# Nine block products split once more, with their inner weight sums made in the first group

## What is computed

```python
# layer 0: one weight for all batches, a low-rank addition chosen by the batch's first id
x = x + (einsum('bsi,oi->bso', x, weight) + bias
         + scale[:, None, None] * einsum('bsr,bor->bso', einsum('bsi,bri->bsr', x, a_sel), b_sel))
# layer 1: the whole weight (2048 x 2048) is chosen by the batch's second id, out of 16
x = x + einsum('bij,bkj->bik', x, w1[id_b])
```

## Time and profile before

| | us |
|---|---|
| median of three runs | 2757.64 |
| the profiled execution | 2755.91 |
| its span in the trace | 2754.1 |
| TensorE busy (share of the span) | 2713.4 (99%) |
| VectorE busy | 1836.7 (67%) |
| ScalarE busy | 1339.2 (49%) |
| GpSimd busy | 732.9 (27%) |
| DMA, mean over the span | 234 GB/s |

### The profile page before, as it was taken

One profiled execution on the slowest core, in us unless ns is written; L12 is line 12 of the kernel. 1 busy time (PEld: TensorE's weight loads), 2 busy tenths in 40 slices (PEclk: granted clock), 3 DMA queues, 4 the chain that ended last, 5 costly groups with the idle time before them and its releaser, 6 DMA issues.

```text
span 2754.1 us, 34174 instructions
## 1 busy us (share of the span) xinstructions
PE 2713.4 (99%) x12042; PEld 2244.8 (82%) x12042; DVE 1836.7 (67%) x1631; ACT 1339.2 (49%) x1409; POOL 732.9 (27%) x589
## 2 busy tenths in 40 slices
PE   6999999999999999999999999999999999999999
PEld 5788888888888888888888888888888888888887
DVE  5766776866655657686656575768675656667865
ACT  3332355756533335576643232666664323366665
POOL 4435812411512111141251210113134122111421
PEclk9999999999999999999999999999999999999999
DMA  7858947666855435666794544899997554499997
GB/s 269 331 188 284 351 167 225 206 222 219 312 173 198 143 129 178 211 221 208 232 310 161 185 156 137 288 305 312 308 326 276 168 180 163 138 303 311 309 321 246
DMA packets 197627, 645.17 MB, mean 234 GB/s; under 512 B 23216, under 2 KB 33616, under 8 KB 197456
## 3 DMA queue, kind: packets, MB, share of 16 engines
q1 hardware_dynamic: 197456, 642.98, 68.6%
HBM read 651.28 MB, written 58.72 MB: 258 GB/s over the span
## 4 chain that ended last, share of the span: by engine, by line
PE 89%; POOL 3%; DMA 3%; DVE 3%; ACT 1%; issue 1%; SPq 0%; POOLq 0%; ACTq 0%; DVEq 0%
PE acc L820 16%; PE acc L821 16%; PE acc L822 16%; PE acc L766 13%; PE acc L777 13%; PE acc L767 13%; DMA raw<-w 3%; POOL raw L493 2%; PE acc L739 2%; DVE ws L710 1%; POOL raw L476 1%; PE acc L775 1%; DMA raw<-xt 0%; DVE ops L710 0%; ACT ws L574 0%
## 5 line engine op out<-in xcount | busy, mean ns | idle before, releaser
L710 DVE TENSOR_TENSOR ws<-raw,ws 128x1024 fp32r<-128x1024 f32 (+1 forms) x1008 | 1317.5, 1330 | 432.9 <-ACT ws L574 428.8
L574 ACT CAST ws<-raw 128x1024 fp32r<-128x1024 f32 (+1 forms) x1008 | 1027.9, 1044 | 1146.7 <-PE acc L777 519.0
L820 PE MATMUL acc<-ws,ops 128*128 128x512 f32 (+1 forms) x2048 | 799.0, 390 | 5.2 <-DVE ws L710 4.8
L821 PE MATMUL acc<-ws,ops 128*128 128x512 f32 (+1 forms) x2048 | 797.9, 390 | 0.0
L822 PE MATMUL acc<-ws,ops 128*128 128x512 f32 (+1 forms) x2048 | 797.9, 390 | 0.0
L766 PE MATMUL acc<-ops,ws 128*128 128x512 f32 x1792 | 702.1, 392 | 19.8 <-DVE ops L710 14.4
L777 PE MATMUL acc<-ops,ws 128*128 128x512 f32 x1792 | 700.9, 391 | 0.0
L767 PE MATMUL acc<-ops,ws 128*128 128x512 f32 x1792 | 699.8, 391 | 0.0
L493 POOL TENSOR_TENSOR raw<-raw,eye_s 128x128 f32<-128x128 f32 x384 | 351.6, 946 | 1261.3 <-DMA raw<-w 1261.3
L820 PEld LDWEIGHTS acc<-ws,ops 128*128 128x128 f32 x2048 | 384.6, 188 | 89.1 <-issue 6.5
L476 POOL TENSOR_TENSOR raw<-raw 128x1024 f32<-128x1024 f32 (+1 forms) x116 | 305.6, 2636 | 555.1 <-DMA raw<-xt 456.5
(11 more groups left out here) (61 smaller groups left out, 651.4 us busy)
## 6 DMA issues: line engine op xcount, KB each, us to landing
raw<-w SPq DMA_DIRECT2D x928, 512.0 KB
raw<-xt SPq DMA_DIRECT2D x176, 512.0 KB
raw<-w_sums SPq DMA_DIRECT2D x104, 512.0 KB
out<-ost SPq DMA_DIRECT2D x128, 256.0 KB, 6.0
w_sums<-raw SPq DMA_DIRECT2D x32, 512.0 KB, 5.3
x_sums<-raw SPq DMA_DIRECT2D x16, 512.0 KB, 4.2
raw<-x_sums SPq DMA_DIRECT2D x16, 512.0 KB
raw<-a SPq DMA_DIRECT2D x80, 64.0 KB
```

Of the source, the lines that this page charges most:

```text
L574: ins = eng.copy(hi, src)
L710: ins = eng.tensor_tensor(lo, src, hi, ALU.subtract) if hi is not None else eng.tensor_copy(lo, src)
L820: eng.matmul(acc, yh, wh, start=begin, stop=False)
L821: eng.matmul(acc, yh, wl, start=False, stop=False)
```

## The change

For `k` in `TWO` = (2, 3, 5) of groups 1, 2 and 3 (nine block products in all) the block product is itself done by seven smaller products `s` of a 2 x 2 form. A small product takes two weight tiles' worth of slots (`("V", g, k, s, hh)`, `hh` = 0, 1); each block has 24 matmuls of 128 x 128 by **256** columns. A product that was 8 blocks of 24 matmuls of 512 columns becomes 14 blocks of 24 matmuls of 256 columns. The low-rank matmuls stay 16 per product (four each within `s` = 1, 2, 6 and four in a new block `LV`).

```diff
+            if two(g, k):
+                for s in range(7):
+                    for hh in range(2):
+                        blocks.append(("V", g, k, s, hh))
+                    if s == 5:
+                        blocks.append(("LV", g, k))
+                continue
...
+                    for o in range(2):
+                        dst = acc[:, 512 * hh + 256 * o:512 * hh + 256 * o + 256]
+                        for t in range(4):
...
+                            eng.matmul(dst, wh, xh, start=fresh, stop=False, skip_group_check=True)
+                            eng.matmul(dst, wh, xl, start=False, stop=False, skip_group_check=True)
...
+                            ins = eng.matmul(dst, wl, xh, start=False, stop=(t == 3), skip_group_check=True)
```

**The inner input sums** are four tiles of 128 x 1024 per product (`("XT", g, k, m)`). POOL makes them in place, from the four raw tiles of the product's X splits, which therefore stay in `raw` until the sums have been split; ACT and DVE split them into the other half of `ops`, once the block product before is done:

```diff
+        return (["T3", "T2"], ["T1"], [], ["T4"])[index[2]]
...
+                elif kind == "XT":
+                    g, k, m = index
+                    x11, x21 = raw[:, 0:2, 0:512], raw[:, 0:2, 512:1024]
+                    x12, x22 = raw[:, 2:4, 0:512], raw[:, 2:4, 512:1024]
+                    if step == "T3":
+                        eng.wait_ge(s_lo, max(number["X", g, k, b] for b in range(G)) + 1)
...
+                        ins = eng.tensor_tensor(x12, x22, x12, ALU.subtract)
```

```diff
+    begin = ts[at["S", 0, 0, 0, 0, 0]]
+    for i, k in enumerate(TWO):
+        for o in range(4):
+            key = begin + 8.0 + 26.0 * (4 * i + o)
+            jobs.append((key, key, "P", (k, o)))
+            for step in range(len(pool_steps("P", (k, o)))):
+                pool_at["P", k, o, step] = key + 3.0 * step
```

**The evictions** of such a product are nine additions of 128 x 1024 (task `evt`: PSUM is now four pairs of banks) instead of eight of 128 x 512:

```diff
+        pair = [ctx.enter_context(nc.psum_tensor(f"acc{i}", [P, 1024], F32)) for i in range(4)]
...
+                    eng.tensor_tensor(dst, acc, src, ALU.add).then_inc(s_ev0, 1)
```

More of the change, by code:

```diff
@@ L9 @@
 ALU = mybir.AluOpType
+ACTF = mybir.ActivationFunctionType
 P = 128
@@ L33, with two @@
 SAVE_AFTER = 5
+TWO = (2, 3, 5)
+def two(g, k):
+    return g > 0 and k in TWO
 def plan_blocks():
@@ L129, in pool_steps, with halves @@
     return []
+def halves():
+    main, first = {}, 0
+    for g in range(NG):
+        half = first
+        for k in range(K):
+            if k and not two(g, k - 1):
+                half = 1 - half
+            main[g, k] = half
+        first = 1 - half
+    return main
 def program(nc, xt, a0, w0, w1, bt, bias, row, col, seq, half, scal, eye, out):
@@ L139, in program @@
         now += LORA_COST if b[0] == "W" and b[2] in (2, 3, 5) else 0.0
+        now += LORA_COST if b[0] == "V" and b[3] in (1, 2, 6) else 0.0
         te.append(now)
-    slots = [b for b in blocks if b[0] in ("W", "LA", "S")]
+    slots = [b for b in blocks if b[0] in ("W", "V", "LA", "S")]
     slot_of = {b: n for n, b in enumerate(slots)}
+    main_half = halves()
     def slot_done(n):
@@ L180, in program @@
                 key = free + 0.3 + (need - free) * (b + 0.2) / 4.6
-                splits.append((key, need, "X", (g, k, b)))
+                jobs.append((key, need, "X", (g, k, b)))
+            if two(g, k):
+                free = te[other_done(g, k)]
+                ready = key + 2.8
+                for m in range(4):
+                    for step, what in enumerate(pool_steps("XT", (g, k, m))):
+                        pool_at["XT", g, k, m, step] = ready
+                        ready += 2.6
+                    jobs.append((max(ready + 0.1, free + 0.4 + 2.6 * m), ts[at["V", g, k, 3 + m, 0]], "XT", (g, k, m)))
         for h in range(2):
@@ L224, in program @@
             split_of[r] = (n, i, what)
[L225 to L233, removed]
+    dadd_no = {number_at["W", 0, 1, o]: o + 1 for o in range(HT)}
     def out_no(g, h, kc, b):
         return ((g * 2 + h) * C1 + kc) * G + b
+    scalar_tasks, vector_tasks, stores = [], [], []
@@ L238, in program, with last_ev @@
+    scalar_tasks.sort(key=lambda t: t[:2])
+    vector_tasks.sort(key=lambda t: t[:2])
+    stores.sort()
+    ev_no = {}
+    for _, _, what, index in vector_tasks:
+        if what in ("ev0", "evt"):
+            ev_no[index] = len(ev_no) + 1
+    def last_ev(g, k, o):
+        return ev_no[g, k, 4 if o < 4 else 8] if two(g, k) else ev_no[g, k, o, 0]
     with ExitStack() as ctx:
@@ L388, in save @@
             def save(n):
-                kind, index = splits[n][2:4]
-                r, _ = saves[n]
+                kind, index = jobs[n][2:4]
                 if n in dadd_no:
@@ L413, in _ @@
                             eng.wait_ge(s_pool, pool_no[m, j])
-                    else:
-                        eng.wait_ge(s_lo, m + 1)
-                        if m in saves:
-                            eng.wait_ge(s_save[place[r]], saves[m][1])
-                if what[0] not in ("w0", "scratch", "t2") and not ordered:
+                    elif kind == "X" and two(*index[:2]):
+                        eng.wait_ge(s_lo, max(number["XT", index[0], index[1], i2] for i2 in range(4)) + 1)
+                    else:
+                        eng.wait_ge(s_lo, number[(kind, *index)] + 1)
+                    if prior[r] in saves:
+                        eng.wait_ge(s_save[place[r]], saves[prior[r]])
+                if what[0] not in ("w0", "scratch", "t2", "w2") and not ordered:
                     ordered = True
@@ L453, in _ @@
                     eng.dma_start(bias_s[:], bias).then_inc(s_const, 16)
-                if n in saves and i + 1 == len(raws[n]):
+                if (saved(kind_, index_) or kind_ == "P") and i + 1 == len(raws[n]):
                     waiting.append(n)
@@ L499, in split_views @@
         def split_views(n):
-            kind, index = splits[n][2:4]
+            kind, index = jobs[n][2:4]
+            if kind == "XT":
+                g, k, m = index
+                i = HT * (1 - half_of(g, k)) + 4 * (m // 2)
+                l, c = ((0, 0), (2, 512), (2, 0), (0, 512))[m]
+                v = raw[:, l:l + 2, c:c + 512].rearrange("p l (t n) -> p t l n", t=4)
+                c = 256 * (m % 2)
+                hi, lo = (ops[:, i:i + 4, w, c:c + 256].rearrange("p t (l n) -> p t l n", l=2) for w in range(2))
+                return [(v, hi)], [(v, hi, lo)]
             if kind == "BS":
```

406 lines of the change are left out of this document (302 added, 104 removed).

## The result

The changed kernel takes 2919.15 us (median of 4 runs, 2917.39 to 2919.69), the kernel before 2757.8 in the same comparison: 1.0585 times as long, 95% interval 1.0567 to 1.0604. The forecast was slower, 2789, with a range to 2832; the loss is five times as large, 161 us for 31.

A forecast was written before the change was run, and what follows sets the result against it. TensorE bounds the old kernel; in split products DVE, with POOL beside it, would. Waits of 60.3 us less 28.8 saved give +31.5 on 2755.9, 2787.4; with 1.7 for the median, 2789 us, range 2724 to 2832.

The forecast's parts named there:

- TensorE: what goes: Split products: 336 matmuls of 256 columns at 0.12 us save 3.2 us each; nine save 28.8, between 2 and 49.
- DVE: what comes, and POOL beside it: Split products: DVE work 38.1 us (k=3) or 45.7 (k=2, 5), plus 1.4 stolen per POOL operation, 11.2 per product.
- The sum: DVE work plus stolen time less 7.9 us, against TensorE's time: 20.1 us of waits per group, 60.3 over three.
- the 7.9 us: How far DVE may fall behind TensorE, by the ring of `ws`, once per run of split products.
- break-even: The whole change breaks even where each POOL operation steals c from DVE: 24c - 13.1 = 9.6 us per group, c = 0.95.
- DVE hides: Rival: in split products POOL operations cost DVE under 0.5 us each, TensorE stays the bound; 2729 us, chance 0.23.
- The rest: ACT, loads, P jobs, first group's slots, stores and new orders outside the split products' sum: hidden or taken as 0.
- The P jobs: Twelve weight-sum jobs, 48 POOL operations, 62 us in some 350, and 25 MB of transfers: hidden, at most some 8 us.
- slots of `raw` bound: Rival: some 20 loads per split product through five slots take up to 51.6 us; +54 over nine, 2812, chance 0.08.

The follow-up runs named there:

- experiment 15: Changed kernel with only k=3 split once more, no P jobs, X's `raw` slots lent to weight loads; 2763.51 us, 1.0028 times the kernel before.
- e14_k3_alone: The run of experiment 15: changed kernel with only k=3 split once more, no P jobs, X's `raw` slots lent; 2763.51 us, 1.0028 times the kernel before.
- the frame: Changed kernel with its new `raw` slots, three output tiles and new orders, but no product split once more and no P jobs; 2788.82 us, 1.0125 times the kernel before.
- e6_lend: The frame with X's four slots of `raw` lent to weight and rank-16 weight loads too; 2760.3 us, 1.0018 times the kernel before.
- e12_best: Changed kernel with X's slots lent, stores earlier, P jobs' POOL steps and saves 6 us later, and `LV` last; 2889.82 us, 1.0484 times the kernel before.
- the frame with the P jobs: The frame plus the twelve P jobs (loads, POOL operations, saves), no product split once more; 2856.87 us, 1.0379 times the kernel before.
- e11_no_xt_sums: Changed kernel without the P jobs (inner weights read from plain weights) and without POOL's four XT sums per product; 2807.65 us, 1.0179 times the kernel before.

## Why the prediction was wrong, step by step

- *TensorE: what goes.* Right. 0.12 us per small matmul, 3.2 us won per product. The bounds were 0.1133 and 0.129; the nearest row was the spacing of two weight loads in the earlier trace rows.
- *DVE: what comes, and POOL beside it.* Right in kind: DVE with POOL beside it fills 93% of k=2 and 3. The eviction at 1.23 was 1.21, the time stolen per POOL operation at 1.4 was 1.3 there and 1.0 in k=5. But eight such operations were counted in each product, and k=2 and 3 have twelve together, k=5 has four. The stolen time was priced at 22.4 and 11.2 us and is 16.0 and 3.9.
- *The sum.* It gave 98.3 us for k=2 and 3 and 49.0 for k=5; measured in group 1 are 99.1 and 50.6. That they meet so closely is luck, for its terms did not hold. In k=2 and 3 DVE is busy for 92.7 us and idle for 6.4, mostly in waits for casts. The busy time is less than the sum's 106.2 because 6.4 us less were stolen and because splits that follow each other start 1.14 us apart though each is 1.22 long (two take 2.28 in the chain shown for experiment 15). The idle time was set at nothing. And the 7.9 us by which DVE was allowed to fall behind do not appear: TensorE waits for an eviction at `LV`, 13.3 of its 19.9 us of waits, and only 6.6 for the low parts in `ws` and `ops`, where the forecast put them all. Over the nine products the net was put at +31.5 and is +42.2. `e14_k3_alone` shows the same from the other side: where the sum says that TensorE stays the bound, it is 2.5 to 4.1 us short.
- The break-even in the rival *DVE hides* has a slip: its own terms give 24c - 13.5, not 13.1, and c = 0.96.
- *The rest* is the step that failed. "The first group has no such products ... it may lose as much again or win it, taken as 0": measured +31.0 in the changed kernel and +22.5 in the frame. It is the slots: with X's lent, the frame loses nothing there (`e6_lend`) and the whole change 1.7 us (`e12_best`). A tile of k=1 takes three of five slots at a time, and that could be counted beforehand.
- The P jobs were "hidden", with at most 8 us: measured +66.5. They were priced as amounts (62 us of POOL in 350, 25 MB of DMA). In the frame with the P jobs, where the loss is 68.9, POOL's time is 14 of it and all that is left at the end 5. What the prediction left out is what stands behind a wait in its queue: SP's wait for POOL before a save, and the stores placed by a fixed planned distance behind it, are 49 us, the stores most of them.
- The blocks around the split products were put at 0 and lose 19.1 us, 8.9 of them by POOL's XT sums before the `LA` splits (by `e11_no_xt_sums`).
- The rival *slots of `raw` bound* had the right object in the wrong place: it priced the split products, where the wait for the next X operand does show in `e14_k3_alone`, and not the first group.

## What to carry to other kernels

A job put beside other work is priced by the queues it stands in, not by its busy time: name for each wait that it adds the engine that issues it and everything issued after it. When a pool of buffers is parted by use, count for each stage how many one item takes at once. And when TensorE's work is cut at the price of more splitting, count for each stage which operations of POOL really fall into it, add the time that DVE loses beside them, and then follow the next operand from the slot it needs to its last split. Where a forecast agrees with the measured time, check its terms too: here they erred by more than the sum.

## What the hardware showed that was not expected

- A stream of matmuls of 256 columns, each with its own weights, runs at 0.120 us and not at half of 0.2267. The second level of splitting thus saves 7% of a product and not the eighth that the count promises. The Trainium skill (TensorE: Matmul & The Clock Gate, Back-to-back issue gap) has 109 ns for one such matmul by itself; in a stream with a weight load for each the measured 120 decides.
- A wait of TensorE of 5.70 us costs more than itself. It comes back at the lower level of its clock: the granted clock is 0.93 over k=2, and the next 19 matmuls are 0.213 us apart instead of 0.120, at 1.2 instead of 2.4 GHz. That is some 2 us more.

```profile
947.26 1.22 PE L1049 MATMUL acc<-lows,bs 128*128 128x256 f32 x4 [5.70 <-DVE cb L918]
948.29 0.41 PE L1035 MATMUL acc<-ops,ws 128*128 128x256 f32 x1
948.50 0.41 PE L1036 MATMUL acc<-ops,ws 128*128 128x256 f32 x1
```

- DVE and POOL both lose when they meet: an X difference on POOL, 2.40 us at the median, takes 3.50 where it starts during DVE's splits, and the P sums of 512 columns take 1.87 us on average where 1.29 is their own time. The Trainium skill (SBUF — State Buffer, Who interferes with whom) has it that the order of issue decides who blocks; the trace agrees, since both are found blocked.

```profile
998.91 3.50 POOL L607 TENSOR_TENSOR raw<-raw 128x1024 f32<-128x1024 f32 x1 [2.58 <-DMA raw<-xt]
L647 POOL TENSOR_TENSOR raw<-raw 128x512 f32<-128x512 f32 x12 | 22.5, 1872 | 0.8
```
